# First rows in halves over two banks, and row statistics joined by aggregate operations, in a feed-forward, attention, feed-forward block

## What is computed

```python
x = x + 0.5 * ffn(layernorm(x), ...)
x = x + attention(layernorm(x), ...)
x = x + 0.5 * ffn(layernorm(x), ...)
```

```python
logits = x @ router_w.T
scores = sigmoid(logits); s = scores + bias
gmask = the 2 best of 4 groups of 4 experts (by the sum of a group's two best s)
topk_idx = the 4 best s in those groups
tw = scores at topk_idx, divided by their sum, times 2.5
h = x @ gate_w[e]; u = x @ up_w[e]
y[e] = (silu(h) * u) @ down_w[e]
out = sum over e of y[e] * combine[:, e]  +  (silu(x @ sh_gate_w) * (x @ sh_up_w)) @ sh_down_w
```

## Time and profile before

| what | us |
|---|---|
| median of 3 runs | 665.79 |
| lowest and highest of them | 665.75, 666.40 |
| the profiled execution | 665.98 |
| its span in the trace | 664.2 |

### The profile page before, as it was taken

One profiled execution on the slowest core, in us unless ns is written; L12 is line 12 of the kernel. 1 busy time (PEld: TensorE's weight loads), 2 busy tenths in 40 slices (PEclk: granted clock), 3 DMA queues, 4 the chain that ended last, 5 costly groups with the idle time before them and its releaser, 6 DMA issues.

```text
span 664.2 us, 10555 instructions
## 1 busy us (share of the span) xinstructions
PE 658.0 (99%) x3169; PEld 550.7 (83%) x3169; DVE 519.2 (78%) x1441; ACT 406.4 (61%) x817; POOL 445.1 (67%) x385
## 2 busy tenths in 40 slices
PE   8999999999999999999999999999999999999997
PEld 7888888888888888888888888888888888888886
DVE  6896969698785977869778788787785968868664
ACT  5876575656666566666567655676566565655554
POOL 6997666666756678565775667766667666666663
PEclk9999999999999999999999999999999999999999
DMA  9816060603307033070240700604207042250700
GB/s 232 276 51 256 5 252 1 242 14 109 148 0 256 1 120 136 1 255 1 88 168 1 245 12 22 249 1 175 97 20 254 0 162 111 60 212 3 270 0 33
DMA packets 30262, 75.38 MB, mean 113 GB/s; under 512 B 3569, under 2 KB 12545, under 8 KB 30209
## 3 DMA queue, kind: packets, MB, share of 16 engines
q1 hardware_dynamic: 30208, 74.74, 31.9%
HBM read 72.11 MB, written 2.62 MB: 113 GB/s over the span
## 4 chain that ended last, share of the span: by engine, by line
PE 98%; DVE 1%; issue 0%; ACT 0%; POOL 0%; DVEq 0%; POOLq 0%
PE gateP L449 10%; PE yP L453 10%; PE yP L449 10%; PE yP L450 10%; PE upP L449 10%; PE gateP L453 10%; PE upP L453 10%; PE gateP L450 10%; PE upP L450 10%; PE prepP L490 2%; PE attP L507 1%; PE prepP L482 1%; PE backP L471 1%; PE yP L578 1%; PE backP L563 1%; PE attP L563 1%
## 5 line engine op out<-in xcount | busy, mean ns | idle before, releaser
L340 POOL TENSOR_TENSOR A_lo<-A,A_hi 128x512 fp32r<-128x512 f32 x287 | 370.1, 1291 | 203.4 <-ACT A_hi L817 203.4
L843 ACT ACTIVATE gateP<-gateP 128x512 f32<-128x512 f32 x252 | 146.6, 582 | 201.9 <-PE gateP L453 201.0
L1160 DVE TENSOR_TENSOR T<-gateP,CB 128x512 f32<-128x512 f32 x252 | 173.2, 687 | 88.5 <-ACT gateP L843 80.7
L817 ACT CAST A_hi<-A 128x512 fp32r<-128x512 f32 x287 | 176.0, 613 | 11.3 <-DVE A L1191 7.8
L1191 DVE TENSOR_TENSOR A<-upP,T 128x512 f32<-128x512 f32 x254 | 175.6, 691 | 8.7
L449 PE MATMUL gateP<-XT_hi,W_hi 128*128 128x512 f32 x288 | 118.6, 412 | 0.0
L449 PE MATMUL yP<-A_hi,W_hi 128*128 128x512 f32 x288 | 112.6, 391 | 0.0
L453 PE MATMUL yP<-A_lo,W_hi 128*128 128x512 f32 x288 | 112.5, 391 | 0.0
L453 PE MATMUL gateP<-XT_lo,W_hi 128*128 128x512 f32 x288 | 112.5, 391 | 0.0
L450 PE MATMUL gateP<-XT_hi,W_lo 128*128 128x512 f32 x288 | 112.3, 390 | 0.0
L450 PE MATMUL yP<-A_hi,W_lo 128*128 128x512 f32 x288 | 112.1, 389 | 0.0
(11 more groups left out here) (231 smaller groups left out, 645.2 us busy)
## 6 DMA issues: line engine op xcount, KB each, us to landing
CB<-combT SPq DMA_DIRECT2D x126, 512.0 KB, 6.9
out_dram<-X SPq DMA_DIRECT2D x7, 256.0 KB, 2.0
X<-in_L_attn_x_dram SPq DMA_DIRECT2D x3, 512.0 KB, 9.4
W_in<-in_L_ffn_gate_w_dram SPq DMA_DIRECT2D x4, 256.0 KB, 5.1
W_in<-in_L_ffn_up_w_dram SPq DMA_DIRECT2D x4, 256.0 KB, 5.1
W_in<-in_L_ffn_down_w_dram SPq DMA_DIRECT2D x4, 256.0 KB, 5.5
X<-in_L_attn_x_dram SPq DMA_DIRECT2D x2, 256.0 KB, 3.1
combT<-CT SPq DMA_DIRECT2D x16, 32.0 KB, 1.8
```

Of the source, the lines that this page charges most:

```text
L340: pool.tensor_tensor(A_lo[:, slot, :], A[:, slot, :], A_hi[:, slot, :].bitcast(F32), ALU.subtract).then_inc(low_done, 1)
L817: act.copy(A_hi[:, v % SLOTS, :], A[:, v % SLOTS, :]).then_inc(high_done, 1)
L843: act.activation(dst, gateP[u % 2][:, :], ACT.Silu).then_inc(silu_done, 1)
L1160: dve.tensor_tensor(T[:, u % TS, :], silu, weights, ALU.mult).then_inc(gate_weighted, 1)
```

## The change

Nothing of what is computed changes; the diff has five parts.

1. **Statistics.** All joins go through BN_AGGR: four of them (one for each 128 rows) turn the six numbers of BN_STATS into mean and variance. In the first block one operation adds epsilon, and the normalisation subtracts the mean instead of adding its negative; elsewhere two operations follow (`nmean`, `vareps`). `aggregate(1)` stands ahead of the first block's normalisation.
2. **Halves.** The first block's transposes go two to `prepP` and two to `backP`; the copy to `XT`, the rounding to `XT_hi` and the first two and last two logits are done by halves of 256 columns. `XT_lo` is made by VectorE for the first half and by GpSimd for the second. The logits go to `attP` in step 0, so `up(2)`, which uses that bank, waits until they are read (`route_seq` of 2).
3. **TensorE's first units.** The gate and up products of unit 0 are interleaved, so that both products with `XT_lo` come last. `gate(5)` moves ahead of the transposes of `comb`, `transpose_weights(0)` to their front, and `up(4)` between `spread(0)` and `spread(1)`. `WARM` is 9 instead of 13, and the two `FILL` after the first transposes are gone.
4. **GpSimd's order.** `W_lo` of unit 0 waits for the normalisation of the first block, then comes the second half of `XT_lo`, then the units 1 to 5, the rstd of the second block, and the units 6 and 7; 8 and 9 now stand between the first `A_lo` (`SPLIT_AT`).
5. **Loads.** `R_in` and `ebias` are issued by ScalarE instead of SP.

```diff
@@ -64,7 +64,7 @@
     SPREAD = 4
-    WARM, FILL = 13, 2
+    WARM, FILL = 9, 2
@@ -252,13 +254,15 @@
         def combine_bank(t):
-            return (upP[0], attP)[t] if isinstance(t, int) and t < 2 else prepP
+            return attP if isinstance(t, int) and t == 1 else prepP
+        def logits_bank(t):
+            return (attP, backP)[t] if isinstance(t, int) and t < 2 else prepP
...
             sp.dma_start(X[:, 0:TILES, :], x_v[0][:, 0:TILES, :]).then_inc(x_first, 16)
-            sp.dma_start(R_in[:, :], router_w).then_inc(router_in, 16)
-            sp.dma_start(ebias[:, :], bias.unsqueeze(0).broadcast_to([P, E])).then_inc(ebias_in, 16)
@@ -386,7 +390,7 @@
             step_rstd(0)
-            SPLIT_AT = {4: 10, 5: 11, 7: 12, 8: 13, 9: 14, 10: 15, 11: 16, 12: 17}
+            SPLIT_AT = {2: 8, 3: 9, 4: 10, 5: 11, 7: 12, 8: 13, 9: 14, 10: 15, 11: 16, 12: 17}
@@ -425,12 +429,19 @@
                                            ALU.add).then_inc(row_added, 1)
-            for unit in range(SHARED):
+            pool.wait_ge(xn_ready, 2)
+            split_low(0)
+            pool.wait_ge(xt_hi_ready, 1)
+            cols = HALVES[1]
+            pool.tensor_tensor(XT_lo[:, 0, cols], XT[:, cols], XT_hi[:, 0, cols].bitcast(F32),
+                               ALU.subtract).then_inc(xt_lo_ready, 1)
+            for unit in range(1, 6):
                 split_low(unit)
-            pool.wait_ge(xn_ready, 2)
             step_rstd(1)
-            for unit in range(SHARED, 10):
+            for unit in range(6, 8):
@@ -484,17 +493,20 @@
             def logits(t):
-                pe.wait_ge(xt_ready, t + 1)
-                bank = backP if isinstance(t, int) and t < 2 else prepP
+                if isinstance(t, int) and t == 0:
+                    pe.wait_ge(xt_copied_half, 1)
+                else:
+                    pe.wait_ge(xt_ready, t + 1)
+                bank = logits_bank(t)
                 for j in range(TILES):
+                    if isinstance(t, int) and t == 0 and j == TILES // 2:
+                        pe.wait_ge(xt_ready, 1)
@@ -594,23 +604,34 @@
                     one(first_up[u], u, 1).then_inc(up_done, 1)
-                gate(0)
-                up(0)
+                pe.wait_ge(w_lo_done, 1)
+                pe.wait_ge(xt_hi_ready, 1)
+                for i, dst in enumerate((gateP[0], first_up[0])):
+                    pe.matmul(dst[:, :], W_hi[:, 0, i, :], XT_hi[:, 0, :], start=True, stop=False)
+                    pe.matmul(dst[:, :], W_lo[:, 0, i, :], XT_hi[:, 0, :], start=False, stop=False)
+                pe.wait_ge(xt_lo_half, 1)
+                pe.wait_ge(xt_lo_ready, 1)
+                for i, (dst, done) in enumerate(((gateP[0], gate_done), (first_up[0], up_done))):
+                    pe.matmul(dst[:, :], W_hi[:, 0, i, :], XT_lo[:, 0, :], start=False,
+                              stop=True).then_inc(done, 1)
...
                 gate(3)
+                pe.wait_ge(route_seq, 2)
...
                 gate(4)
-                pe.wait_ge(route_seq, ROUTE_OPS)
+                gate(5)
+                transpose_weights(0)
                 spread(0)
+                pe.wait_ge(mul_done, 1)
+                up(4)
+                pe.wait_ge(ct_ready, 1)
                 spread(1)
-                transpose_weights(0)
-                gate(5)
-
-                pe.wait_ge(ct_ready, 1)
-                up(4)
@@ -691,8 +712,12 @@
             keep_busy(FILL)
-            transpose_next(0)
-            keep_busy(FILL)
+            for h, (bank, done) in enumerate(((prepP, xt_half), (backP, xt_done))):
+                pe.wait_ge(xn_ready, h + 1)
+                for j in range(TILES // 2):
+                    mm = pe.transpose(bank[:, j * P:(j + 1) * P], XN[:, h * TILES // 2 + j, :], ident[:, :])
+                mm.then_inc(done, 1)
@@ -852,9 +877,10 @@
                     if first and u in (3, 4):
+                        if u == 3:
+                            copy_weights(0)
...
                         if u == 3:
-                            copy_weights(0)
@@ -877,6 +903,8 @@
                         attention_stage(u, p - ATT0)
+            act.dma_start(R_in[:, :], router_w).then_inc(router_in, 16)
+            act.dma_start(ebias[:, :], bias.unsqueeze(0).broadcast_to([P, E])).then_inc(ebias_in, 16)
@@ -884,7 +912,9 @@
                 split_high(unit)
-            next_high(0, 0)
+            for cols, copied, done in zip(HALVES, (xt_copied_half, xt_ready), (xt_hi_half, xt_hi_ready)):
+                act.wait_ge(copied, 1)
+                act.copy(XT_hi[:, 0, cols], XT[:, cols]).then_inc(done, 1)
...
-                dve.tensor_scalar(within, sums[:, :, 1], 1.0 / P, EPS, ALU.mult, ALU.add).then_inc(stats_seq, 1)
-                dve.wait_ge(stats_seq, base + 3)
-                dve.scalar_tensor_tensor(parts[:, 1, :], parts[:, 0, :], 0.25, diffp, ALU.mult,
-                                         ALU.mult).then_inc(spread_square, 1)
-                dve.wait_ge(spread_square, count)
-                dve.tensor_tensor(vareps[:, :], parts[:, 1, :], within, ALU.add).then_inc(stats_seq, 1)
+            def aggregate(t, dst):
+                dve.wait_ge(stats_seq, 4 * t + 1)
+                for j in range(TILES):
+                    ins = dve.bn_aggr(dst[:, j, :], bst[:, j, :])
+                ins.then_inc(stats_seq, 1)
             def stats(t):
-                merge_stats(stats_seq, 4 * t, bst, nmean[:, :], vareps[:, :], parts)
+                dve.wait_ge(stats_seq, 4 * t + 2)
+                dve.tensor_scalar(nmean[:, :], mv[:, :, 0], -1.0, None, ALU.mult)
+                dve.tensor_scalar(vareps[:, :], mv[:, :, 1], EPS, None, ALU.add).then_inc(stats_seq, 2)
@@ -1210,10 +1215,8 @@
                     if w == (13 if early else 12) and not last:
-                        if early:
-                            stats_in_psum(2, prepP[:, FREE_AT:FREE_AT + 4 * TILES], 2)
-                        else:
-                            stats(t0 + s + 2)
+                        aggregate(t0 + s + 2, mv)
+                        stats(t0 + s + 2)
@@ -1225,41 +1228,27 @@
             rows(0, 0)
-            stats(0)
+            aggregate(0, first_mv)
+            dve.wait_ge(stats_seq, 2)
+            dve.tensor_scalar(vareps[:, :], first_mv[:, :, 1], EPS, None, ALU.add).then_inc(stats_seq, 2)
...
             rows(1, 1)
+            aggregate(1, mv)
...
             for j in range(TILES):
-                ins = dve.tensor_scalar(XN[:, j, :], X[:, j, :], nmean[:, j:j + 1], rstd[:, j:j + 1],
-                                        ALU.add, ALU.mult)
+                ins = dve.tensor_scalar(XN[:, j, :], X[:, j, :], first_mv[:, j, 0:1], rstd[:, j:j + 1],
+                                        ALU.subtract, ALU.mult)
...
                     ins.then_inc(xn_ready, 1)
-
-
-            sums = attP[:, 0:2 * TILES].rearrange("p (j c) -> p j c", c=2)
-            diffp, within = attP[:, 2 * TILES:3 * TILES], attP[:, 3 * TILES:4 * TILES]
-            both = bst[:, :, :].rearrange("p j (h c) -> p j c h", h=2)[:, :, 1:3, :]
-            dve.wait_ge(setup_sb, 1)
-            dve.wait_ge(stats_seq, 5)
-            dve.tensor_reduce(sums, both, AX.X, ALU.add).then_inc(stats_seq, 1)
-            dve.wait_ge(stats_seq, 6)
-            for dst in (parts[:, 0, :], diffp):
-                dve.scalar_tensor_tensor(dst, bst[:, :, 1], 2.0, sums[:, :, 0], ALU.mult, ALU.subtract)
-            dve.tensor_scalar(nmean[:, :], sums[:, :, 0], -0.5, None, ALU.mult)
-            dve.tensor_scalar(within, sums[:, :, 1], 1.0 / P, EPS, ALU.mult, ALU.add).then_inc(stats_seq, 1)
-
-            dve.wait_ge(xt_done, 1)
-            dve.tensor_copy(XT[:, :], prepP[:, :]).then_inc(xt_ready, 1)
-
-            dve.wait_ge(stats_seq, 7)
-            dve.scalar_tensor_tensor(parts[:, 1, :], parts[:, 0, :], 0.25, diffp, ALU.mult,
-                                     ALU.mult).then_inc(spread_square, 1)
-            dve.wait_ge(spread_square, 1)
-            dve.tensor_tensor(vareps[:, :], parts[:, 1, :], within, ALU.add).then_inc(stats_seq, 1)
-
-            dve.wait_ge(xt_hi_ready, 1)
-            dve.tensor_tensor(XT_lo[:, 0, :], prepP[:, :], XT_hi[:, 0, :].bitcast(F32),
-                              ALU.subtract).then_inc(xt_lo_ready, 1)
+            for cols, bank, made, done in zip(HALVES, (prepP, backP), (xt_half, xt_done),
+                                              (xt_copied_half, xt_ready)):
+                dve.wait_ge(made, 1)
+                dve.tensor_copy(XT[:, cols], bank[:, HALVES[0]]).then_inc(done, 1)
+                if bank is prepP:
+                    stats(1)
+            dve.wait_ge(xt_hi_half, 1)
+            dve.tensor_tensor(XT_lo[:, 0, HALVES[0]], prepP[:, HALVES[0]],
+                              XT_hi[:, 0, HALVES[0]].bitcast(F32), ALU.subtract).then_inc(xt_lo_half, 1)
...
```

(3 more changed lines are left out.)

41 lines of the change are left out of this document (6 added, 35 removed).

## The result

| | before | after |
|---|---|---|
| median of 7 runs each, one chip | 665.86 us | 668.38 us |
| lowest to highest | 665.75 to 666.4 | 667.27 to 669.42 |
| profiled execution: time, span | 665.98, 664.2 (at the prediction) | 667.27, 665.6 |

The ratio is 1.0034, 95% interval [1.0024, 1.0043]: slower, by more than the 0.2% that a measurement can tell. I had forecast 665.05, and 0.07 for slower. Beside the experiments the changed kernel was timed again on another chip: 667.26 against 665.87, ratio 1.0027 [1.0018, 1.0036].

What follows compares the result with a forecast made beforehand. TensorE was taken to bound the kernel, with GpSimd's `A_lo` cutting its possible gain of 1.6 us to 0.7 at unit 3's down product; later steps gave nothing. Median 665.79 less 0.75 gave 665.05, range 664.2 to 666.6.

Steps and rivals of the forecast that it cites:

- chain 1: From the span's start to TensorE's first gate product: it starts at about 9.1 instead of 10.25, 1.15 us earlier.
- The gain of 0.7 at the down product of unit 3: GpSimd's `A_lo` of unit 3 ends at 25.8, so this product starts at 25.85 instead of 26.56, not 1.6 earlier.
- the second routing keeps pace: VectorE in step 0: lighter by the third block's statistics, so the second routing is not late; no time of its own.
- The clock rival: Shorter warm-up: TensorE's rise from 1.2 to 2.4 GHz comes late; 665.8 to 667.1 or more; chance 0.12, half beyond 667.1.
- that rival: BN_AGGR dear, 0.87 for four instead of 0.42: all three chains start 0.8 to 0.9 later, 665.8 to 665.9; chance 0.12.
- GpSimd's half: GpSimd's new second half of `XT_lo`, 256 columns, ahead of the later `W_lo`: 0.7 us, between 0.6 and 0.9 possible.
- The routing's transposes: TensorE at the first routing's end: comes at 16.2, finds `comb` there, the 0.64 hole goes; gain about 1.6 us.
- The wait for an `A_lo` at unit 2: Sign to look for: TensorE waits for `A_lo` at the down products of units 2 and 3, 0.3 to 1 us together.
- the sum itself: Whole kernel: the 0.7 gained at unit 3's down product stays to the end; 0.75 off the median gives 665.05 us.

Runs made afterwards that it cites:

- experiment 1: Changed kernel with BN_AGGR's mean and variance of the second and third block in PSUM banks instead of SBUF: 665.66 us, ratio 0.9995 to the kernel before.
- experiment 2: Kernel before with only the short warm-up (`WARM` 9, no products of ones behind the first transposes): 666.61 us, ratio 1.001; its profiled execution took 667.8.
- experiment 4: Kernel before with only the second and third block's statistics made by BN_AGGR into SBUF: 666.96 us, ratio 1.0015.
- experiment 5: Last version: changed kernel, both blocks' statistics in banks, fill behind the first transposes, low weight parts of units 8 to 17 later: 665.59 us, ratio 0.9994.

## Why the prediction was wrong, step by step

**The step that failed** is in chain 1: "VectorE copies half 1, does two small operations and copies half 2". I priced the two at what small operations cost alone and had both halves copied by 8.5. The first of them waited for GpSimd's `W_lo`. From the start of the first to the copy behind them they took 0.64 (8.03 to 8.67; 0.13 in experiment 1, 7.90 to 8.03), and half 2 was copied by 9.08. Everything behind followed: `XT_hi` complete at 9.52 (forecast 8.9), first gate product at 9.66 (9.1), and GpSimd's wait for `XT_hi` 0.94 (0.4), so its half of `XT_lo` started 0.7 later than forecast, and `A_lo` of unit 3 ended at 26.53 instead of 25.8. Of these 0.73, 0.54 are the longer wait and 0.16 a `W_lo` that began at 7.66 instead of 7.5. The gain of 0.7 at the down product of unit 3 was gone there: +0.03.

**The second failure** is the sentence "On VectorE step 0 gets lighter by the statistics of the third block, so the second routing keeps pace". Seven small operations with their sums in a bank took 0.91 before, from 42.34 to the start of `T` at 43.25, and the new ones took from 42.48 to 44.63, 2.15. TensorE waited behind them, and the stretch cost 1.1.

What both missed was where the sources lie, and what GpSimd does at that time. The kernel before put these sums in `attP` and `prepP`; I read that as a detail. A row to be read for it was in the trace of before, outside my groups: the first operation of `merge_stats`, with both sources in SBUF, took 0.17 for the same 4 columns in the first block, beside an idle GpSimd, and 0.24 to 0.37 in the 13 later steps, each time beside an `A_lo`. The group, and one of the later steps:

```profile
L906 DVE TENSOR_TENSOR parts<-bst x14: 166/350/366, 4.5 to 571.1; 128x4 f32<-128x4 f32 x14
...
115.79 1.28 POOL L340 TENSOR_TENSOR A_lo<-A,A_hi 128x512 fp32r<-128x512 f32 x1 [0.74 <-ACT A_hi L817]
...
116.74 0.36 DVE L906 TENSOR_TENSOR parts<-bst 128x4 f32<-128x4 f32 x1
```

The spread of one shape was the sign.

**The clock rival** I gave 0.12, and half of it beyond 667.1. A loss through the clock came in 5 of 7 and 5 of 11 runs, at 1.1 a group, not in one of eight. Whether it is the rival's mechanism, a late first rise, stays open: one trace shows that (experiment 2, 1.86), but the mean clock of the slower runs points behind the rise. Then the argument that holes and waits of 0.3 to 0.6 leave the upper level in place, read from one execution, would be what failed.

**What held.** BN_AGGR: 0.38 for four, 0.42 taken, so that rival falls. GpSimd's half: 0.74 for 0.7. The routing's transposes found `comb` there, and TensorE was 1.1 ahead behind them (at the down product of unit 0), where the forecast was 1.6: short by the 0.56 by which the first gate product was late. The wait for an `A_lo` at unit 2 was there, 0.6. And the sum itself holds for the kernel of experiment 1, in which the failed steps don't occur: gate product at 9.03 (9.1), wait of GpSimd 0.46 (0.4), `A_lo` of unit 3 at 24.61 + 1.28 = 25.89 (25.8), TensorE 0.61 ahead at the first product of unit 3's down product and 0.50 at its second (0.7). It stays at 0.50 past the third block's transposes (48.23 against 48.72), and 0.37 are left at the end; the steps between are small, and I have no cause for them. Its median is 0.3 below the kernel before, where I had 0.75. So even without the failed steps the gain is half of what I had, inside what a measurement can't tell from no change.

**Sum of the result**: 668.38 - 665.86 = 2.5. The two runs at a clock of 1.000 (667.27 and 667.32) are 1.4 above the kernel before: about 1.6 for the stalls, less 0.3 that the rest of the change wins. The other 1.1 are the median run's lower clock. The 1.6 is measured on other chips than the 1.4, and good to 0.3.

## What to carry to other kernels

Before small VectorE operations are moved from PSUM to SBUF, look at what GpSimd does at that time: where it has no room, an operation of 0.15 can cost as much as GpSimd has left, and everything queued behind it pays. Price an operation by place and not by shape alone; a maximum far above the median of a group is the row to look for. When warm-up work is shortened, one profile doesn't do: read the clock of every run, and the spacing of the matmuls in the profile.

## What the runs showed of the hardware

- **A `tensor_scalar` of 128x4 from SBUF to SBUF waits for GpSimd**: 0.32, 0.51, 0.55, 0.66, 0.74, 1.18 and 1.75 to 1.79 us beside a GpSimd that streamed from SBUF, 0.17 beside an idle one, 0.15 to 0.16 with its source in a bank. The Trainium skill (SBUF — State Buffer, Who interferes with whom) says that VectorE's copies and `tensor_scalar` in a two-port mode and GpSimd take one port pair in turn, and that the later one blocks fully. The trace agrees; by that rule I should have had both stalls.
- The wait **can outlast one instruction of GpSimd**. Of the `A_lo` x2 at 42.09 the first ends at about 43.4 (half of 2.53), 0.5 after `nmean` began, but `nmean` ended with the second, at 44.64. The Trainium skill (SBUF — State Buffer, Who interferes with whom) says that the pair is held for the whole instruction; here it was not handed over between two that followed without a pause. Four profiled executions ended so (in each, `nmean` began 0.8 after the first `A_lo`), and none has a third instruction in a row there. A fifth case went the other way: in experiment 4 `nmean` began 0.5 into the first of two `W_lo` and ended with it, at 9.69, and the operation behind it took 0.16 beside the second. What decides between the two is open.
- The mean granted clock of a run, 0.997 or 0.996 instead of 1.000, goes with 0.8 to 1.3 us. It leaves out the time before the first rise (experiment 2): there the spacing must be read. The Trainium skill (TensorE: Matmul & The Clock Gate, Part 1) has the rise at another place from run to run. The traces agree: the spacing of the products halves at 4.9 us in experiment 4, at 6.6 in the kernel before and at 14.5 in experiment 2.
- GpSimd's `A_lo` of the first 45 us took 1.28 to 1.32 on average in the profiled executions, 1.28 in experiment 1 and 1.32 in the last version of experiment 5. I didn't follow that up.
